# Sums of four states instead of pairs in the scan of a four-block fused kernel, and PE's collecting products at other places

## The reference, cut to what matters

```python
# block 2: 16 heads of 128, softmax over the context
q = rmsnorm((x @ Wq).reshape(B, Sq, H, D), gq)
k = rmsnorm((ctx @ Wk).reshape(B, Skv, H, D), gk)
attn = softmax(einsum('bqhd,bkhd->bhqk', q, k) * scale)
out = einsum('bhqk,bkhd->bqhd', attn, v).reshape(B, Sq, H * D) @ Wo

# block 3: the scan, 16 states n for each of 512 channels d
def step(state, inp):
    d, b, c, u = inp
    dA = exp(d[..., None] * A)
    state = state * dA + (d * u)[..., None] * b[:, None, :]
    y = einsum('bdn,bn->bd', state, c)
    return state, y
y = y + D[None, :, None] * x
```

## Time and profile before

| | |
|---|---|
| median of 3 runs | 4372.96 us |
| lowest and highest | 4348.32 and 4377.12 us |
| the profiled execution | 4363.04 us |
| its span, first to last instruction | 4361.3 us |
| mean granted TensorE clock | 0.884 of full speed |
| busy in the span: PE, DVE, ACT, POOL | 3474.4, 2804.6, 1529.8, 1127.1 us |
| the scan stage, first to last scan step | 1868.8 to 3515.6 us |

### The profile page before, as it was taken

The page is one execution under the profiler, slowest core; times in us unless marked ns, Lnnn a source line. Parts: engine busy times, 40 slices in busy tenths (PEclk is TensorE's granted clock), DMA queues, the critical chain, the costliest instruction groups (busy, mean ns, idle before and its releaser), DMA issues. The chain is left out here.

```text
span 4361.3 us, 43119 instructions
## 1 busy us (share of the span) xinstructions
PE 3474.4 (80%) x13573; PEld 1992.5 (46%) x13604; DVE 2804.6 (64%) x3929; ACT 1529.8 (35%) x2449; POOL 1127.1 (26%) x854
## 2 busy tenths in 40 slices
PE   6787677777778865499999999999998779999816
PEld 3474332323235541244444444444444358878613
DVE  4346747474758865477777877777778733236578
ACT  1232434242535435333334333333333311126400
POOL 0102020202000001154444444445544412422200
PEclk9888898988989987689999999989999869999958
DMA  1243303121171000333333343334333351337521
GB/s 60 96 144 126 97 18 88 35 70 55 51 158 13 1 26 30 109 117 116 119 120 116 119 137 116 113 114 132 120 121 114 98 119 44 114 128 250 195 94 38
DMA packets 208828, 428.53 MB, mean 98 GB/s; under 512 B 31456, under 2 KB 33120, under 8 KB 201970
## 3 DMA queue, kind: packets, MB, share of 16 engines
q1 hardware_dynamic: 201298, 407.05, 30.9%
q0 software_dynamic: 6240, 16.81, 1.0%
q10 hardware_dynamic: 1088, 2.10, 0.2%
HBM read 347.95 MB, written 81.59 MB: 98 GB/s over the span
## 5 line engine op out<-in xcount | busy, mean ns | idle before, releaser
L1943 POOL TENSOR_TENSOR l2x_inflow<-l2x_dtu,l2x_rows_b 128x512 f32<-128x512 f32 x256 | 393.2, 1538 | 505.9 <-DVE l2x_state L1823 374.4
L1646 ACT ACTIVATE l2x_probs<-psum,l2x_soft,l2x_norms 128x512 f32<-128x512 f32 x256 | 195.7, 774 | 599.0 <-DVE l2x_soft L1749 599.0
L1823 DVE TENSOR_TENSOR_SCAN l2x_state<-l2x_decay,l2x_inflow 128x512 f32<-128x512 f32 x256 | 384.4, 1502 | 27.4 <-ACT l2x_decay L1689 18.2
L179 POOL TENSOR_TENSOR ln_work<-ln_work,minus_half 128x4 f32<-128x4 f32 x33 | 33.4, 1013 | 1393.0 <-DVE ln_work L167 1393.0
L943 DVE TENSOR_REDUCE l1x_mx<-psum 128x2 f32<-128x1024 f32 x256 | 308.5, 1223 | 59.5 <-PE psum L797 58.6
L126 PE MATMUL psum<-l2x_probs_t,l2x_v_tok 128*128 128x512 f32 x512 | 276.1, 689 | 87.9 <-DVE l2x_probs_t L212 50.5
L905 ACT ACTIVATE l1x_k_split<-psum 128x1024 f32<-128x1024 f32 x256 | 248.6, 1023 | 195.9 <-PE psum L797 195.3
L218 DVE SCALAR_TENSOR_TENSOR x_res<-psum,gate,x_res 128x512 f32<-128x512 f32 (+1 forms) x144 | 106.8, 749 | 267.4 <-PE psum L126 260.0
L1832 DVE TENSOR_TENSOR l2x_state<-l2x_state,l2x_rows_c 128x512 f32<-128x512 f32 x256 | 233.7, 913 | 23.2 <-DMA l2x_rows_c<-l3x_xd_dram 19.2
L126 PE MATMUL psum<-l2x_kt,l2x_qt 128*128 128x512 f32 x512 | 230.2, 592 | 0.0
L797 PE MATMUL psum<-l1x_ks,l1x_qs 48*128 48x512 f32 x512 | 135.6, 531 | 115.4 <-ACT l1x_k_split L905 69.4
(11 more groups left out here) (392 smaller groups left out, 7386.8 us busy)
## 6 DMA issues: line engine op xcount, KB each, us to landing
l2x_rows_b<-l3x_xd_dram SPq DMA_DIRECT2D x256, 256.0 KB, 3.7
l2x_rows_c<-l3x_xd_dram SPq DMA_DIRECT2D x256, 256.0 KB, 3.8
l2x_wq<-l_wq SPq DMA_DIRECT2D x16, 1024.0 KB, 7.1
l2x_wo<-l_wo SPq DMA_DIRECT2D x16, 1024.0 KB, 5.2
l2f_xs_dram<-l1f_empty SPq DMA_DIRECT2D x1, 11799.0 KB, 87.8
l2r_xs<-l2f_xs_dram SPq DMA_DIRECT2D x23, 513.0 KB, 3.8
l2r_raw<-l_w SPq DMA_DIRECT2D x11, 1024.0 KB, 7.1
l2w_raw<-l_w SPq DMA_DIRECT2D x10, 1024.0 KB, 7.4
```

Of the source, the lines that this page charges most:

```text
L1646: ring.drain(act.activation(probs[:, h % 2, t, :], bank(f"s{u}_{h}_{t}"), ACT.Exp, bias=soft[:, h % 2, 1, t:t + 1], scale=norms[:, u % 2, ...
L1823: dve.tensor_tensor_scan(state[:, s % KEPT, :], decay[:, s % 3, :], inflow[:, s % 3, :], 0.0, ALU.mult, ALU.add).then_inc(scan_done, 1)
L1943: pool.tensor_tensor(inflow[:, s % 3, :], dtu[:], rows_b[:, s % 3, :], ALU.mult).then_inc(inflow_ready, 1)
```

## The change

POOL adds each second pair onto the pair before it, right behind that pair, so that four states stand in one sum (a new semaphore `four_added`, since the addition reads what POOL's last one wrote). PE collects four such sums a unit in place of eight pairs. Their places are: 3 (of the unit before) within the keys of u + 1, 0 after score 2, 1 after turn 2, 2 after the values of u + 1 and ahead of the keys' transposes. The waits of the scan and of the skip term count the new groups. Nothing else differs; the other lines only have other numbers, six less on POOL's helpers.

```diff
--- before.py
+++ after.py
@@ -1425,7 +1425,7 @@
              "k_scaled", "q_ms", "q_norm", "pool_steps", "max_ready", "bias_ready", "inv_ready", "probs_ready")]
         (dtu_ready, decay_ready, inflow_ready, scan_done, gathered, y_filled, y_read) = [sem(n) for n in (
             "dtu_ready", "decay_ready", "inflow_ready", "scan_done", "gathered", "y_filled", "y_read")]
-        paired = sem("paired")
+        paired, four_added = sem("paired"), sem("four_added")
         dt_in, u_loaded, y_out = [[sem(f"{n}{k}") for k in range(2)] for n in ("dt_in", "u_loaded", "y_out")]
         b_in, c_in = [[sem(f"{n}_in{k}") for k in range(3)] for n in "bc"]
         ln = LayerNorm(g, sem)
@@ -1592,48 +1592,42 @@
 
             def collect(u, m):
                 if u >= 0:
-                    k = u * NS // 2 + m
-                    pe.wait_ge(paired, k + 1)
+                    k = u * NS // 4 + m
+                    pe.wait_ge(four_added, k + 1)
                     if m == 0:
                         since(pe, y_read, u)
-                    pe.matmul(y_bank, g["ident"][:], state[:, 2 * k % KEPT, :], start=(m == 0),
-                              stop=(m == NS // 2 - 1)).then_inc(y_filled, 1)
+                    pe.matmul(y_bank, g["ident"][:], state[:, 4 * k % KEPT, :], start=(m == 0),
+                              stop=(m == NS // 4 - 1)).then_inc(y_filled, 1)
 
             for u in range(-1, NU):
                 score(u, 0)
-                collect(u - 1, 6)
                 x_turned(u + 1)
                 context(u + 1, "k", wk, wk_in, (0, 1))
-                collect(u - 1, 7)
+                collect(u - 1, 3)
                 context(u + 1, "k", wk, wk_in, (2, 3))
                 score(u, 1)
                 query(u + 1, 0)
                 query(u + 1, 1)
-                collect(u, 0)
                 turn(u, 0)
                 value(u, 0)
                 turn(u, 1)
-                collect(u, 1)
                 score(u, 2)
+                collect(u, 0)
                 value(u, 1)
                 query(u + 1, 2)
-                collect(u, 2)
                 score(u, 3)
                 query(u + 1, 3)
                 turn(u, 2)
-                collect(u, 3)
+                collect(u, 1)
                 value(u, 2)
                 query_norms(u + 1)
                 turn(u, 3)
-                collect(u, 4)
                 value(u, 3)
                 context(u + 1, "v", wv, wv_in, range(ST))
+                collect(u, 2)
                 keys_turned(u + 1)
-                output(u, (0, 1))
-                collect(u, 5)
-                output(u, (2, 3))
-            collect(NU - 1, 6)
-            collect(NU - 1, 7)
+                output(u, range(ST))
+            collect(NU - 1, 3)
 
         @blk.scalar
         def _(act):
@@ -1819,7 +1813,7 @@
                     s = u * NS + n
                     dve.wait_ge(decay_ready, s + 1)
                     dve.wait_ge(inflow_ready, s + 1)
-                    since(dve, y_filled, (s - KEPT) // 2 + 1)
+                    since(dve, y_filled, (s - KEPT) // 4 + 1)
                     dve.tensor_tensor_scan(state[:, s % KEPT, :], decay[:, s % 3, :], inflow[:, s % 3, :], 0.0, ALU.mult,
                                            ALU.add).then_inc(scan_done, 1)
 
@@ -1833,7 +1827,7 @@
 
             def skip_term(u):
                 if u >= 0:
-                    dve.wait_ge(y_filled, (u + 1) * NS // 2)
+                    dve.wait_ge(y_filled, (u + 1) * NS // 4)
                     tile = u_in[:, u % 2, :]
                     dve.scalar_tensor_tensor(tile, tile, g["skip"][:, u % G2:u % G2 + 1], y_bank, ALU.mult,
                                              ALU.add).then_inc(y_read, 1)
@@ -1950,6 +1944,10 @@
                     pool.wait_ge(gathered, s + 1)
                     even = state[:, (s - 1) % KEPT, :]
                     pool.tensor_tensor(even, even, state[:, s % KEPT, :], ALU.add).then_inc(paired, 1)
+                    if n % 4 == 3:
+                        pool.wait_ge(paired, (s + 1) // 2)
+                        first = state[:, (s - 3) % KEPT, :]
+                        pool.tensor_tensor(first, first, even, ALU.add).then_inc(four_added, 1)
 
             for u in range(-1, NU):
                 for n in range(NS):
```

## The result

The changed kernel takes 4439.3 us, median of 4 runs (4433.2 to 4448.9), against 4374.6 us for the kernel before beside it (4 runs): a ratio of 1.0159, 95% interval 1.012 to 1.0199. It is slower by 65 us. The forecast was 4420, within 4365 to 4455.

The account below looks back on a forecast made before the run. Each unit was bound by PE in stretch B and DVE in stretch A. From the profiled 4363: 15 x 3.3 = +49.5, last unit +1, PE -3, clock +8 gave 4419, say 4420 us; range 4365 to 4455.

Parts of the forecast that it names:

- A: Stretch of a unit from the end of the output products to value 2: PE waits, DVE sets the pace.
- B: Stretch of a unit from value 2 to the end of the output products: DVE waits, PE sets the pace.
- old 4: Removed collect between turn 3 and value 3, ahead of a 0.53 us wait for DVE: worth 0.
- The -3: One collect fewer after score 0: 0.86 us gained in each of 3 units where x is turned, taken as -3.
- Sums 2 and 3: POOL's additions behind pairs 11 and 15, where DVE waits for PE: cost 0.
- Sum 0: POOL's addition behind pair 3: delays key norms and inflow 8, so scan 8 ends 2.2 us later (or 1.1).
- sum 1: POOL's addition behind pair 7: a fourth POOL operation among the four key scalings, +1.1 us a unit.
- The clock: PE's longer idle time, with value 2 already slow: +0.5 us a unit, +8 in all, ends -15 and +47.
- Rival 1: PE is the bound after all, whole kernel: 4308 us if all is paid back, 4336 for half; chance 0.12.
- rival 2: Sums stay covered in the scan stage; only key scalings pay: 4377, or 4360 with nothing; chance 0.18.
- rival 4: The change doesn't shorten PE's list of instructions; no size or chance given.
- Rival 3: Clock pays too: all units lose what the 107.1 us one does, 47 us instead of 8: 4458; chance 0.14.

Follow-up runs that it names:

- e1: Kernel before plus POOL's four sums a unit, written to a spare tile nobody reads; PE collects eight pairs as before: 4431.8 us, 1.0136.
- e3: Kernel before plus only the sum behind the pair that ends with state 3, to a spare tile: 4406.2 us, 1.0096.
- e4: Kernel before plus only the sum behind the pair that ends with state 7, to a spare tile: 4379.9 us, 1.0012.
- e7: Kernel before with collect 5 moved from between the output products to behind score 0 of the next unit: 4356.7 us, 0.9957.
- e2: Changed kernel without POOL's sums; PE collects only the first pair of each four, leaving out half of y's sum: 4382.3 us, 1.0029 to before.
- e10: Kernel before plus only the sums behind pairs 11 and 15, to a spare tile: 4375.2 us, 0.9999.
- e9: Changed kernel with collect 2 put back between turn 3 and value 3: 4401.4 us, 1.0067 to the kernel before.
- e6: Kernel before plus only the sum of pair 3, issued behind the three key-norm steps: one run, 4379.0 us.
- e8: Kernel before with query product 3 made twice and turn 2's last transposes four times, where PE waited: 4365.1 us, 0.9969.
- e11: Kernel before with both e7's moved collect and e8's repeated PE work: 4344.0 us, 0.9939.

## Why the prediction was right, and where it wasn't

- **Bound by stretches.** Right. A follows DVE (e1, e3, e4), B follows PE (e7), and busy shares would have misled: e2 has 55 us less of PE's work and no gain.
- **The collects place by place.** Right for all but one: A's four, old 4 and old 5 gave 0 (A in e2 63.25, shortest B 38.05 in both kernels); but old 4 was worth 0 at full clock only, as said below. The -3 for the units where x is turned did not show: with three units shorter by 0.86, e2's mean A would be 63.06, and it is 63.25. The three units themselves have 64.2, 63.7 and 64.6 us before and 63.9, 63.7 and 64.7 in e2.
- **Sums 2 and 3 at 0.** Right (e10). Sum 2 did hold a normalisation: the wait at the query norms went from 5.49 to 4.48 us, so the cover was used up by 1 us and held.
- **Sum 0 at +2.2, sum 1 at +1.1.** Right in mechanism, step by step; 3.3 was 3.55. From scan 5's end, scan 8 ended 2.50 us later, and the end of the scalings another 1.06. Inflow 8 ended 2.55 us later, where the prediction had 1.2 to 2.3. It had missed two things that pull against each other: the first key-norm step is no longer held (-0.45), and the third, taken as 2.91 us, took 3.40, with gather 7 (2347.77) beside its start. The rest of A, 3.62 in all, is 0.08 us before scan 5.
- **The last unit at +1.** 1.0.
- **The new waits at 0.** Right: the collects after show no idle time before them, and scan 8's wait was for its inflow, not for collect 0.
- **The clock at +0.5 a unit, +8.** Right in sign and near in size, but with the wrong place behind it, so the size is in part luck. Between the two profiled executions B grew by 1.02 a unit, 15 us. Between the medians the difference is 64.7 us, of which A and the last unit are 15 x 3.62 + 1 = 55.3, so that some 9 are left. Which of the two it is can't be said, since B's mean varies by execution (e10). The step that failed is the reason: the prediction looked only at PE's longer idle time ahead of value 2, and had old collect 4, ahead of value 3, at nothing. With A's idle time alone (e1) the longest B stays at 43.6. What is new is value 3.

PE's timeline shows it. After, a unit in the lower clock:

```profile
2271.57 4.23 PE L1581 MATMUL psum<-ones,l2x_q_sq 128*128 128x1 f32 x32
2275.66 3.65 PE L119 MATMUL psum<-ident,l2x_probs 128*128 128x128 f32 x16
2280.10 5.94 PE L126 MATMUL psum<-l2x_probs_t,l2x_v_tok 128*128 128x512 f32 x8 [0.79 <-DVE l2x_probs_t L212]
```

and before, such a unit:

```profile
2145.41 4.34 PE L1581 MATMUL psum<-ones,l2x_q_sq 128*128 128x1 f32 x32
2149.61 3.65 PE L119 MATMUL psum<-ident,l2x_probs 128*128 128x128 f32 x16
2153.06 1.91 PE L1599 MATMUL psum<-l2x_state,ident 128*128 128x512 f32 x2
2154.76 3.69 PE L126 MATMUL psum<-l2x_probs_t,l2x_v_tok 128*128 128x512 f32 x8
```

And the granted clock (the third number from the right; the columns are those of the windows above) around value 3 in the same two units. Before:

```profile
2148.20:2154.80 6.60, 6.60 (x27) 5.52 (x27) 4.01 (x6) 1.80 (x3) 4.59 (x3) 0.50 0.16 40
2155.10:2158.30 3.20, 3.20 (x9) 1.33 (x8) 3.17 (x3) 0.00 (x0) 3.12 (x2) 1.00 0.50 164
```

After:

```profile
2274.70:2281.50 6.80, 6.01 (x24) 5.05 (x24) 4.66 (x7) 1.80 (x3) 5.24 (x3) 0.50 0.16 41
2281.50:2284.70 3.20, 3.20 (x5) 1.18 (x4) 3.17 (x2) 0.00 (x0) 3.12 (x3) 0.51 0.46 154
```

Before, old collect 4 stands in front of value 3, PE has no wait there, the clock is back as value 3 begins, and it takes 3.69 us. After, the collect is gone, PE waits 0.79 us, the clock stays low, and value 3 takes 5.94. Over the fifteen units value 3 takes 5.4 us or more in 7 units of after and 8 of e2, and never more than 4.1 in any kernel that has a collect there. A B of 44.9 to 45.0 occurs in 6 of 15 units of after and one of 44.6 or more in 5 of e2, and in none of a kernel that has a collect there; with it put back the longest is 42.8 (e9). So old collect 4, "worth 0", was worth 0 at full clock only, and up to 1.4 us less than nothing in a unit at the lower one. Why the clock comes back later without it is not shown: less work and a new wait go together in these runs.

- **Rival 1** (PE is the bound) fell by e2, **rival 2** (sums covered) by e1, **rival 4** by the 118 records of collects. **Rival 3** was half right. Its mark was a clock below 0.92 with units above 109 us: the clock is 0.88, and the mean unit is 108.6, with 6 of 15 above 109 (110.0 to 112.7). The mark was a poor one, since e1, with none of the new value 3 in it, has 0.91. The clock paid, but some 9 to 15 us, not 47.
- The rest of the marks: scan 8 waits 1.50 us for inflow 8 and has a row of 2.22; the scalings take 6.77 (6.8 was said); the wait of turn 2 is 3.82 us in the unit that is shown here below (5 was said; the fifteen units have 3.7 to 6.5, 4.3 in the mean); collects 256 to 128 records in all, 236 to 118 in the first fifteen units.

In PE's timeline of that unit:

```profile
2367.08 1.97 PE L119 MATMUL psum<-ident,l2x_probs 128*128 128x128 f32 x8 [3.82 <-DVE l2x_probs L1752]
2371.17 1.97 PE L119 MATMUL psum<-ident,l2x_probs 128*128 128x128 f32 x8 [2.12 <-ACT l2x_probs L1640]
...
2376.76 5.41 PE L126 MATMUL psum<-l2x_probs_t,l2x_v_tok 128*128 128x512 f32 x8 [1.91 <-ACT l2x_probs_t L212]
```

Left open is a kernel that really uses e6's finding: sums of four with more state slots, so that a sum can be put off to a place where DVE waits.

## What to carry to other kernels

Moving work from one engine to another pays only where the first is waited for, and costs where the second one's queue is: cut the round into stretches by who waits for whom, and price each moved instruction at its place (sum 0 cost 2.6 us, 1.2 behind the key norms, and sums 2 and 3 nothing). Count POOL's operations that read SBUF as time of DVE whenever both have a queue (seen here for scans, products of two tiles and the normalisation), and ask what the instruction behind the added one will now run beside. A product that fills a wait is not waste by itself; taking it out can make its neighbours slower.

## What was not expected of the hardware

- A POOL operation of 128x16 is held for as long as a large one: a step of 0.22 us took 1.07 beside a scan of 128x512, and one of 2.91 us took 3.40 with a gather beside its start.
- The memsets took 0.52 us each and neither held DVE nor were held.
- With 118 records less, PE was as long busy as before (1420.6 and 1422.6 us), since its granted clock fell. Both halves of the change lower it: 0.94 before, 0.91 with the sums alone, 0.90 with PE's shorter list alone, 0.88 with both. And more work in waiting time (e8, e11) made the kernel faster: 0.97 in e11.
